# Experts' results in a row for each of a token's eight choices, instead of added into three sums

## What is computed

```
topk_idx, topk_w = _route(x, gate_weight, e_bias)      # eight of 64 experts for each token
xe = zeros((E, CAP, H)).at[sorted_e, pos].set(tok_sorted, mode='drop')   # CAP = 128 slots for each expert
h  = silu(einsum('ech,efh->ecf', xe, w1)) * einsum('ech,efh->ecf', xe, w3)
ye = einsum('ecf,ehf->ech', h, w2)
out = segment_sum(vals * flat_w[:, None], flat_t, num_segments=T)        # a token's up to eight results
return out + shared                                     # shared: a dense expert for every token
# outside: x = x + layernorm(that)
```

## Time and profile before

| | us |
|---|---|
| median of 3 runs (lowest, highest) | 1156.87 (1156.38, 1160.2) |
| the profiled execution's own time | 1155.2 |
| its span, first to last instruction | 1153.3 |
| TensorE busy | 860.1 (75%) |
| DVE busy | 793.0 (69%) |
| ACT busy | 688.6 (60%) |
| POOL busy | 592.7 (51%) |

### The profile page before, as it was taken

The page is one execution under the profiler, slowest core; times in us unless marked ns, Lnnn a source line. Parts: engine busy times, 40 slices in busy tenths (PEclk is TensorE's granted clock), DMA queues, the critical chain, the costliest instruction groups (busy, mean ns, idle before and its releaser), DMA issues. The chain is left out here.

```text
span 1153.3 us, 16169 instructions
## 1 busy us (share of the span) xinstructions
PE 860.1 (75%) x5014; PEld 271.3 (24%) x5090; DVE 793.0 (69%) x1222; ACT 688.6 (60%) x1409; POOL 592.7 (51%) x734
## 2 busy tenths in 40 slices
PE   4557999999999999999999999999855510655400
PEld 2321222222222222222222222222213300444300
DVE  7887888889889889989988988988502410111117
ACT  4624777777787787777777778778753100322204
POOL 5730010223457456555645645645656754588847
PEclk9867999999999999999999999999986765766555
DMA  4794432012311122220001221000000110777545
GB/s 102 230 275 87 109 85 60 14 40 66 91 40 32 40 71 59 60 47 6 5 15 40 44 60 20 8 12 8 5 12 15 38 30 26 177 144 142 80 116 194
DMA packets 121643, 77.97 MB, mean 68 GB/s; under 512 B 51743, under 2 KB 105499, under 8 KB 121558
## 3 DMA queue, kind: packets, MB, share of 16 engines
q1 hardware_dynamic: 97782, 67.42, 21.7%
q0 software_dynamic: 21504, 6.79, 5.0%
q10 hardware_dynamic: 2272, 2.73, 1.0%
HBM read 38.75 MB, written 54.95 MB: 81 GB/s over the span
## 5 line engine op out<-in xcount | busy, mean ns | idle before, releaser
L215 DVE TENSOR_REDUCE half_max<-s_pair 128x2 f32<-128x1024 f32 x512 | 602.0, 1218 | 76.1 <-PE s_pair L204 70.3
L1245 ACT ACTIVATE probs<-st_bank 128x512 f32<-128x512 f32 x1024 | 543.7, 602 | 163.9 <-PE st_bank L1305 151.7
L1113 POOL DMA_INDIRECT table<-rows,keys_i x256 | 256.7, 1003 | 179.1 <-issue 68.5
L1305 PE MATMUL st_bank<-q_stack,k_stack 98*128 98x512 bf16 (+1 forms) x948 | 303.9, 387 | 18.5 <-ACT probs L1245 9.6
L1314 PE MATMUL pv_bank<-probs,values 128*9 128x512 f32 x2048 | 268.0, 595 | 7.8 <-ACT unit_out L1179 2.8
L204 PE MATMUL s_pair<-k_stack,q_stack 64*128 64x512 bf16 x1024 | 203.0, 396 | 27.0 <-DVE half_max L215 23.1
L204 PEld LDWEIGHTS s_pair<-k_stack,q_stack 64*128 64x128 bf16 x1024 | 49.2, 93 | 342.7 <-issue 196.4
L1488 POOL DMA_INDIRECT sums<-out,ids x64 | 99.7, 1558 | 39.8 <-ACT out L1543 20.1
L1305 PEld LDWEIGHTS st_bank<-q_stack,k_stack 98*128 98x128 bf16 (+1 forms) x1024 | 77.9, 97 | 169.7 <-issue 84.3
L1502 DVE CAST ids<-xe 128x4 uint32<-128x4 f32 x16 | 2.9, 184 | 135.6 <-DMA sums<-out,ids 83.9
L1007 POOL CAST shift<-minus_max 128x16 bf16<-128x16 f32 x32 | 6.5, 202 | 98.3 <-DVE minus_max L221 98.2
(11 more groups left out here) (181 smaller groups left out, 767.7 us busy)
## 6 DMA issues: line engine op xcount, KB each, us to landing
table<-blank SPq DMA_DIRECT2D x8, 772.0 KB, 7.2
xe<-table SPq DMA_DIRECT2D x16, 386.0 KB, 5.2
q_stack<-q_image SPq DMA_DIRECT2D x96, 64.0 KB
k_stack<-k_image SPq DMA_DIRECT2D x96, 64.0 KB
s<-sums SPq DMA_DIRECT2D x24, 256.0 KB, 6.2
k_image<-k_piece SPq DMA_DIRECT2D x16, 256.0 KB, 3.0
table<-rows,keys_i POOLq DMA_INDIRECT x256
sums<-zeros SPq DMA_DIRECT2D x16, 256.0 KB
```

What stands on the lines that cost most here:

```text
L215: nc.vector.tensor_reduce(halves[:, h:HG:SIDE_HEADS, tile, half], stacks.s_pair[slot % S_SLOTS][:].rearrange("p (s k) -> p s k", s=SIDES), ...
L1113: pool.indirect_dma_start(out=table, out_offset=bass.IndirectOffsetOnAxis(ap=keys_i[c % 2][:, pick:pick + 1], axis=0), in_=rows[c % 2][:, ...
L1245: A.activation(probs[:, s % P_SLOTS, :], st_bank[at % ST_BANKS][:], ACT.Exp).then_inc(bank_free, 1)
L1305: M(bank(at)[:], k_stack[g][own, tile // PER, h, tile % PER * P:(tile % PER + 1) * P], q_stack[g][own, half, h, :], start=True, stop=True) ...
```

## The change

- The three sums become one array `results` in DRAM with a row for each token and choice, 8 x 4096 rows of 128 values (16.8 MB). Each slot's result is written to its own row by a plain indirect DMA, with no order among them. It is cleared in units 9 to 12 and 17 to 20, a DMA of 2 MB each, from a larger tile of zeros; the first three small clears, the 16 clears of sums and the eight stores of the shared result are gone.
- The row's number is eight times the token's number plus a rank. DVE finds the rank by counting, among the weights in the slot, those of later experts that are chosen. So that these can be told from the others, routing adds -1 to the weights of experts that aren't chosen (one more DVE instruction for each chunk), empty slots hold -1, and a constant masks the expert itself and those before it (`behind`).
- In `run_experts` DVE has three instructions for ids where it had one, on 64 columns for each expert in the first round and four in the last. The waits on adds become waits on the plain writes (`put`), three rounds before as until now.
- In `finish` SP loads 2 MB for each chunk: eight rows for each token. DVE sums four of them by one reduce over a view with the choice innermost; TensorE, idle there until now, adds the other four and the shared result (still in SBUF) by multiplying with the identity, into a PSUM bank; DVE adds bank and sum. The rest is as before, but works in place.

The diff, cut to its core (arguments and allocations that only pass the new names are left out):

```diff
@@ -549,10 +549,12 @@
+NOT_CHOSEN = -1.0
 SLOT_ROWS = E * CAP
-ROWS = N + CAP
+RESULT_ROWS = N * TOPK
 BIG = 1e30
-SUMS = 3
@@ -624,7 +626,7 @@
         unit_out = sb("unit_out", [P, CHUNK])
-        zeros = sb("zeros", [P, DIM])
+        zeros = sb("zeros", [P, PER * DIM])
         blank = sb("blank", [P, ROW])
@@ -723,7 +725,8 @@
         PUT = 16 * SIDES * SHIFT_ROWS
-        CLEARS = SUMS * (CHUNKS + 1)
+        CLEAR_AT = [n for n in range(CHUNKS, ALL_UNITS) if n % UNITS in (1, 2, 3, 4)][:CHUNKS]
@@ -773,8 +776,6 @@
                     sp.wait_ge(zeros_done, 1)
-                    for s in sums:
-                        sp.dma_start(s[N:ROWS, :], zeros[:]).then_inc(cleared, 16)
                     sp.wait_ge(setup_done, SETUP)
@@ -782,17 +783,14 @@
                                      blank[:].rearrange("p (o d) -> p o d", o=1).to_broadcast([P, experts, ROW])).then_inc(blanked, 16)
-                elif CHUNKS <= n < 2 * CHUNKS:
-                    for s in sums[1:]:
-                        sp.dma_start(s[(n - CHUNKS) * CHUNK:(n - CHUNKS + 1) * CHUNK, :].rearrange("(t p) d -> p t d", p=P),
-                                     zeros[:].rearrange("p (o d) -> p o d", o=1).to_broadcast([P, PER, DIM])).then_inc(cleared, 16)
+                elif n in CLEAR_AT:
+                    width, run = PER * TOPK * DIM, PER * DIM
+                    first = CLEAR_AT.index(n) * width
+                    sp.dma_start(results.rearrange("(p r) d -> p (r d)", p=P)[:, first:first + width].rearrange("p (o i) -> p o i", i=run),
+                                 zeros[:].rearrange("p (o i) -> p o i", o=1).to_broadcast([P, width // run, run])).then_inc(cleared, 16)
             move_out(ALL_UNITS - 1)
             spread_reciprocals(CHUNKS - 1)
-            for c in range(CHUNKS):
-                sp.wait_ge(s_kept, c + 1)
-                sp.dma_start(sums[0][0:N, :].rearrange("(p t) d -> p t d", p=P)[:, c * PER:(c + 1) * PER, :],
-                             k["shared"][:, c * PER:(c + 1) * PER, :]).then_inc(cleared, 16)
-            sp.wait_ge(cleared, 16 * CLEARS)
+            sp.wait_ge(cleared, 16 * CHUNKS)
@@ -889,7 +887,11 @@
                                        in1=wrec[:].rearrange("p (j o) -> p j o", o=1).to_broadcast([P, PER, E]),
-                                       op0=ALU.mult, op1=ALU.mult).then_inc(weights_done, 1)
+                                       op0=ALU.mult, op1=ALU.mult).then_inc(dve_step, 1)
+                steps += 1
+                dve.wait_ge(dve_step, steps)
+                V.scalar_tensor_tensor(out=rows[c % 2][:, :, DIM:ID], in0=chosen[:], scalar=NOT_CHOSEN, in1=rows[c % 2][:, :, DIM:ID],
+                                       op0=ALU.add, op1=ALU.add).then_inc(weights_done, 1)
@@ -965,12 +967,13 @@
                 nonlocal made
-                G.memset(blank[:], 0.0).then_inc(setup_done, 1)
+                G.memset(blank[:, 0:DIM], 0.0).then_inc(setup_done, 1)
+                G.memset(blank[:, DIM:ID], NOT_CHOSEN).then_inc(setup_done, 1)
                 G.memset(ones16[:], 1.0).then_inc(setup_done, 1)
...
                 pool.wait_ge(later_in, 16 * len(later))
-                pool.wait_ge(setup_done, 4)
+                pool.wait_ge(setup_done, 5)
                 G.tensor_copy(blank[:, ID:ROW], k["spare_id"][:]).then_inc(setup_done, 1)
@@ -1446,6 +1449,7 @@
         h = two(sb, "h", [P, 2 * P])
+        behind, behind_count = sb("behind", [P, Q, E]), sb("behind_count", [P, Q])
         psX, psH, psY = two(ps, "psX"), two(ps, "psH"), two(ps, "psY")
@@ -1453,14 +1457,13 @@
         out_ready = sem("out_ready")
-        added = [sem(f"added{v}") for v in range(SUMS)]
+        ranked, put = sem("ranked"), deep(sem, "put")
...
-        def adds_of(engine, r):
-            for v in range(SUMS):
-                engine.wait_ge(added[v], 16 * ((Q * (r + 1) - 1 - v) // SUMS + 1))
+        def put_of(engine, r):
+            engine.wait_ge(put[r % DEEP], 16 * Q * (r // DEEP + 1))
@@ -1481,13 +1484,12 @@
                 for q in range(Q):
-                    n = r * Q + q
-                    pool.wait_ge(out_ready, n + 1)
-                    if n >= SUMS:
-                        pool.wait_ge(added[n % SUMS], 16 * (n // SUMS))
-                    pool.indirect_dma_start(out=sums[n % SUMS], out_offset=bass.IndirectOffsetOnAxis(ap=ids[a][:, q:q + 1], axis=0),
-                                            in_=out[a][:, q, :], in_offset=None, compute_op=ALU.add).then_inc(added[n % SUMS], 16)
-            adds_of(pool, ROUNDS - 1)
+                    pool.wait_ge(out_ready, r * Q + q + 1)
+                    pool.indirect_dma_start(out=results, out_offset=bass.IndirectOffsetOnAxis(ap=ids[a][:, q:q + 1], axis=0),
+                                            in_=out[a][:, q, :], in_offset=None,
+                                            bounds_check=RESULT_ROWS - 1, oob_is_err=False).then_inc(put[a], 16)
+            for r in range(ROUNDS - DEEP, ROUNDS):
+                put_of(pool, r)
@@ -1497,9 +1499,15 @@
                 if r >= DEEP:
-                    adds_of(dve, r - DEEP)
+                    put_of(dve, r - DEEP)
                     dve.wait_ge(out_ready, Q * (r - DEEP + 1))
-                V.tensor_copy(ids[a][:], xe[a][:, :, ID]).then_inc(slot_read, 1)
+                mine = r * Q
+                V.scalar_tensor_tensor(out=behind[:, :, mine:E], in0=xe[a][:, :, DIM + mine:ID], scalar=0.0,
+                                       in1=consts["behind"][:].rearrange("p (q e) -> p q e", q=Q)[:, :, 0:E - mine], op0=ALU.is_ge, op1=ALU.mult).then_inc(ranked, 1)
+                dve.wait_ge(ranked, 2 * r + 1)
+                V.tensor_reduce(behind_count[:], behind[:, :, mine:E], AX.X, ALU.add).then_inc(ranked, 1)
+                dve.wait_ge(ranked, 2 * r + 2)
+                V.scalar_tensor_tensor(out=ids[a][:], in0=xe[a][:, :, ID], scalar=float(TOPK), in1=behind_count[:], op0=ALU.mult, op1=ALU.add).then_inc(slot_read, 1)
@@ -1538,7 +1546,7 @@
                 if r >= DEEP:
-                    adds_of(act, r - DEEP)
+                    put_of(act, r - DEEP)
                 for q in range(Q):
@@ -1591,21 +1599,25 @@
-def finish(nc, x1, sums, out):
+def finish(nc, consts, results, out):
...
         sem = lambda name: ctx.enter_context(nc.semaphore(name))
-        s = [sb(f"s{v}", [P, TILES, DIM]) for v in range(SUMS)]
-        whole, res = sb("whole", [P, TILES, DIM]), sb("res", [P, TILES, DIM])
+        x1, shared, ident = consts["x1"], consts["shared"], consts["ident"]
+        ADDED = TOPK // 2
+        rows = [sb(f"choices{c}", [P, PER, TOPK, DIM]) for c in range(CHUNKS)]
+        whole = sb("whole", [P, TILES, DIM])
         stats, mv = sb("statsE", [P, TILES, 6]), sb("mvE", [P, TILES, 2])
...
         minus_half = sb("minus_halfE", [P, PER])
+        bank = [ctx.enter_context(nc.psum_tensor(f"sum_bank{a}", [P, CHUNK], F32)) for a in range(2)]
...
         stored = sem("storedE")
-        whole_done, stats_done, mv_done = sem("whole_done"), sem("stats_doneE"), sem("mv_doneE")
+        part_done, bank_done, whole_done, stats_done, mv_done = sem("part_done"), sem("bank_done"), sem("whole_done"), sem("stats_doneE"), sem("mv_doneE")
         half_made, pool_step, less_done = sem("half_madeE"), sem("pool_stepE"), sem("less_doneE")
@@ -1615,25 +1627,39 @@
         def _(sp):
+            width = PER * TOPK * DIM
             for c in range(CHUNKS):
-                for v in range(SUMS):
-                    sp.dma_start(s[v][:, tiles(c), :], sums[v][0:N, :].rearrange("(p t) d -> p t d", p=P)[:, tiles(c), :]).then_inc(loaded[c], 16)
+                sp.dma_start(rows[c][:].rearrange("p t k d -> p (t k d)"),
+                             results.rearrange("(p r) d -> p (r d)", p=P)[:, c * width:(c + 1) * width]).then_inc(loaded[c], 16)
             for c in range(CHUNKS):
                 sp.wait_ge(res_done, c + 1)
-                sp.dma_start(out[c * CHUNK:(c + 1) * CHUNK, :].rearrange("(t p) d -> p t d", p=P), res[:, tiles(c), :]).then_inc(stored, 16)
+                sp.dma_start(out[c * CHUNK:(c + 1) * CHUNK, :].rearrange("(t p) d -> p t d", p=P), whole[:, tiles(c), :]).then_inc(stored, 16)
             sp.wait_ge(stored, 16 * CHUNKS)
+        @block.tensor
+        def _(pe):
+            M = nc.tensor.matmul
+            for c in range(CHUNKS):
+                if c >= 2:
+                    pe.wait_ge(whole_done, c - 1)
+                to = bank[c % 2][:].rearrange("p (t d) -> p t d", t=PER)
+                M(to, ident[:], shared[:, tiles(c), :], start=True, stop=False)
+                pe.wait_ge(loaded[c], 16)
+                for r in range(ADDED, TOPK):
+                    mm = M(to, ident[:], rows[c][:, :, r, :], start=False, stop=(r == TOPK - 1))
+                mm.then_inc(bank_done, 1)
...
             def sum_and_stats(c):
-                dve.wait_ge(loaded[c], 16 * SUMS)
```

(17 more changed lines are left out.)

14 lines of the change are left out of this document (7 added, 7 removed).

## The result

| | before | after |
|---|---|---|
| median of the runs (lowest, highest), us | 1156.72 (1152.99, 1160.2), 8 runs | 1167.63 (1163.17, 1172.9), 8 runs |
| profiled execution's own time | 1155.2 | 1168.9 |
| its span | 1153.3 | 1167.1 |

The ratio is 1.0093, with a 95% interval of 1.0064 to 1.0122: slower by 0.9%, where 1.3% faster was forecast. The forecast for a profiled execution was 1140.4; the one measured took 28.5 us more.

The account below looks back on a forecast made before the run. TensorE was taken to bound attention, POOL's scatter issue the experts and finish. Scatters -39.9, routing and clearing +1, finish +24.1 sum to -14.8 us: 1140.4 profiled, 1142 median; range 1135 to 1149, to 1157 with rival 1.

Parts of the forecast that it names:

- The scatters' price: Experts' stretch: plain scatters cost 0.98 us each, 1.284 apart, as the table scatters do; 39.9 us less.
- Rival 4: Experts' scatters keep today's 1.86 us because POOL's time comes from the write, not the add: 1179 us; chance 0.05.
- POOL's issue stays the bound: Experts' rounds: POOL's four scatters, 5.14 us, set the round; mathematics, DVE and buffers keep up.
- a margin of 1.6 us a round: Experts' buffers: round r+3's results ready 8.7 us after round r's issue ended; POOL asks after 10.3.
- a late landing: Experts' scatters: a landing more than 1.6 us later than the 4.0 us taken would be paid every few rounds.
- The mathematics, put at 4.53: Experts' rounds: down projections of two early rounds start 4.53 us apart at the low clock, under POOL's 5.14.
- Routing: Attention: one more DVE instruction per chunk, 0.47 us kind, mostly hidden as TensorE bounds; 1 us, ends 0 and 4.
- The clears: Attention: eight 2 MB DMAs, 5.4 us of transfer each, fit in 13.5 us of cover on SP's queue; cost nothing.
- rival 1: Finish: DVE's strided reduce takes 4.5 us, not 2.3, and paces it; 11.3 us more, 1153.4 us; chance 0.24.
- the row used: Finish: load rate of 387 GB/s, from this kernel's own finish; 16.8 MB of loads take 43.4 us.
- Rival 2: Finish: TensorE stays at 1.2 GHz, 8.5 us a chunk; 23.4 us over the forecast finish, 1165.5 us; chance 0.08.
- rival 3: Finish: loads run at only 288 GB/s, 7.3 us a chunk, so the gain is gone, 1157 us; chance 0.05.

Follow-up runs that it names:

- run 3: Changed kernel with three of each round's four scatters left out, loads, mathematics and counting kept: 1120.35 us, first to last scatter 56.3 us.
- run 8: Changed kernel with a 128-element memset and its wait on POOL before each scatter: 1193.93 us, scatters 1.97 us apart, first to last 124.2 us.
- run 15: Changed kernel without the -1 for unchosen experts and with contiguous adds in the finish, on another chip: 1138.21 us, ratio 0.9838 to the kernel before.
- run 5: Kernel before with its scatters writing instead of adding, its waits, three arrays and finish kept, no counting: 1131.82 us, ratio 0.9772.

## Why the prediction was wrong

**The scatters' price was right.** 0.98 us each and 1.284 apart, in every run. Rival 4 (they stay at 1.86) is out.

**The step that failed is "POOL's issue stays the bound".** It gave 81 us and a margin of 1.6 us a round. In both profiles of the changed kernel, on two chips, the rounds took 97.2, because results of TensorE reach ScalarE 1.35 to 3.6 us late while POOL issues scatters close together; three such delays in every second round use up more than the margin. This is 16.3 of the 28.5 missed microseconds, and no rival named it. That the scatters are needed is shown (runs 3 and 8), that the chip matters too (run 15); how the one acts on the other isn't. The forecast had looked for a late landing. The profile of before shows no late reader in its settled rounds, with 1.86 us between scatters; but in attention, behind the very scatters from which the price was taken, it shows six. The working itself was sound, as run 15 shows with 81.0 us. The mathematics, put at 4.53, went at 3.75 once free and at a granted clock of 0.92, and the counting's three instructions cost 0.30, 0.29 and 0.16 us at the median (at most 0.47 each was said) beside the path.

**Routing was mis-sized.** Taken 1 us with ends of 0 and 4; it cost 4.8. The reason given was that TensorE bounds that stretch. But the instruction was no 0.47 us one:

```profile
L893 DVE SCALAR_TENSOR_TENSOR rows<-chosen,rows x8: 425/832/999, 274.4 to 920.2; 128x256 f32<-128x256 bf16 x8
```

0.83 us is its median. It stands ahead of the reductions of the scores, which attention waits for, and the units in which it sits, one in four and the last, are 0.2 to 1.2 us longer than before. An engine with 15% free time in the mean had none where the instruction stood. The clears cost nothing, as forecast. Another 2.4 us is how late the first unit happened to start, and 0.6 came after the last.

**After the last scatter** there are 7.0 us to the first load instead of 5.0, 2 us that the forecast left out. With plain scatters in the old frame (run 5) it was so too, and with one scatter a round only 3.1; what takes the time wasn't tried.

**The finish was rival 1, at a smaller price.** The strided reduction takes 3.67 us: not the 2.3 taken, nor the 4.5 of the rival; 1.79 ns an element, where the reduction of scores has 1.19. The finish rose by 3.2 us only, because the loads were quicker than forecast, 421 to 426 GB/s instead of 387. The rule of the Trainium skill, "SBUF — State Buffer", Door 1: The DMA port swizzle, that each access to a new line pays, fits this trace, and contiguous adds over the same four rows took 2.07 us; that the new lines are the reason, and not something else about a strided read, no run tells. And the 425 GB/s of the Trainium skill, "DMA: Bandwidth & Descriptors", Measured, was the better guide than the row used: 387 came from a stretch with stores and 2 KB runs in it, which may be the difference. Rival 2 came true for chunk 0 alone; rival 3 is out.

**The chances.** All of the range hung on one chain of waits computed from rows of an unhurried kernel. Slower had a chance of 0.16, and none of the mechanisms behind it decided it; a slip of the rounds' pace through something unseen had none.
